# A four-layer graph stack on one core: second-layer products that share a stationary operand made one product of 256 columns

## The chip, the core and the metric

One NeuronCore of a Trainium2 chip runs the whole program. The metric is the device time of one execution in microseconds. The kernel before has a median of 750.35 us over three runs (749.72 to 751.56); lower is better.

## What is computed

The input is 64 graphs of 128 nodes with 128 features, `x`, and their adjacency matrices `adj`. Four residual layers follow each other, each after a layer norm and a ReLU: a gated recurrent graph network (five steps of message, aggregation and GRU cell), a gated graph convolution, a sum of five small graph convolutions on 25 nodes, and one normalised graph convolution. The change touches the second of them:

```
h     = relu(layernorm(x))
norm  = (sum(|adj|, -1) + 1e-6) ** -0.5
f_hom = (adj @ ((h @ theta) * norm)) * norm
f_het = h @ W_h
gate  = sigmoid(h @ W_t + b_t)
x     = x + elu(gate * f_hom + (1 - gate) * f_het)
```

The kernel uses (adj scaled) @ h first and theta afterwards, so that each graph needs four things of its normalised h (`xn`, nodes on partitions): its turn (features on partitions), the neighbour sum s = xn.T @ adjT (already turned), then h @ W_t and h @ W_h from the turned h, and s @ theta.

## The kernel before

The 64 graphs are taken in 4 rounds of 16; a round has 4 quads of 4 graphs, and 4 graphs of 128 columns fill one PSUM bank of 512 fp32 columns. The recurrent layer is the backbone: 80 steps (4 rounds, 5 layers, 4 quads), each with nine products of 512 columns on the stored state and nine on the message side, in three banks (R, Z and H or I), and the turning and aggregation of the next step's state. Each step n has two slots, 2n and 2n+1. All else is laid beside the recurrence of the next round by a table of slots: `due(slot, lead, at)` says which quad of which round a piece of work is due for. So the second layer of round r runs beside the first steps of round r+1: `turn_and_sum` (slots 0, 2, 4, 6 of that round, TURN1 = 0) and `l1_linear` (slots 1, 3, 5, 7, LINEAR1 = 1). The second layer of the last round has no recurrence beside it; it runs in a tail, where `keep_busy` (L444) puts products that nobody reads in front of waits.

Each engine has its own program and works through it strictly in the written order, with semaphores between them. On TensorE a step is: state products H, R, Z (L404 to L407), turn of the next state (L391), the even slot's work, message products R, Z, I, aggregation (L400), the odd slot's work. `turn_and_sum` stands in the even slot and `l1_linear` in the odd one.

Before the change a quad of the second layer goes like this:

- TensorE, `turn_and_sum` (L460): 4 transposes of 128 columns into the A bank (L470), then 4 fp32 products xn.T @ adjT of 128 columns into the B bank (L478). Both use the same stationary operand, `xn` of the graph. An fp32 product that is not a transpose is two instructions in the trace (a group "x8" is 4 products).
- ScalarE, `l1_read_turned` (L748): copies A to `hT` (L751) and B to `sT` (L755).
- TensorE, `l1_linear` (L482): a bias product of 512 columns into the C bank (L492), 4 products h @ W_t on top (L495), 4 products h @ W_h into A (L499), 4 products s @ theta into B (L504). L495 and L499 use the same stationary operand, `hT` of the graph.
- ScalarE, `l1_read_linear` (L757): tanh of C to `gate_th` (L762), copy of A to `hetS` (L764). Then, two slots on, `l1_exp` (L766).
- VectorE: `l1_difference` (L1195, `diff` from B and `hetS`), `l1_gate` (L1207, `gated` and `mix`), `l1_finish` (L1217). VectorE also does the `residual` of a later quad (L1181, x_res and its statistics), and the GRU arithmetic (L1359, L1362, L1352, L1335, L1343, L1348).
- GpSimd: the power of the layer norm (L936 to L946), the low halves of the state (L952, L956), `adjT` and `adjTI` scaled (L968, L992), and one large power a round (L984, `dis`).

ScalarE normalises a quad in two halves (`norm_relu`, L713), one in an even and one in an odd slot; the odd half stands behind `l1_read_linear` and `l1_exp` in its program, and the turn of that quad on TensorE waits for it.

Of the kernel before, what the change touches and what calls it, by code (L numbers as in the profile page):

```python
# [15 lines left out]
QUAD = 4  # L16
# [19 lines left out]
def graph_stack(nc, x, adj, nodemask, conv_w, w_ih, w_hh, b_ih, b_hh, theta, W_h, W_t, b_t,  # L36
# [26 lines left out]
    with ctx:  # L63
        ctx.enter_context(nc.allow_non_contiguous_dma("small transposed loads at the start"))

        def sb(name, shape, dt=f32):
# [21 lines left out]
            for n in ("fw", "fmax", "fexp", "fsum", "finv", "fshare", "b2_share"))  # L88
# [5 lines left out]
        adjT = sb("adjT", [128, RG, 128])  # L94
# [13 lines left out]
                                          for n in ("var_eps", "neg_mean", "rstd", "shift"))  # L108
# [13 lines left out]
        sT, gate_th, hetS, diff, gated, neg, ex = (sb(n, [128, 512]) for n in  # L122
                                                   ("sT", "gate_th", "hetS", "diff", "gated", "neg", "ex"))
# [28 lines left out]
            "fexp_done", "bias_rows_made",  # L152
# [183 lines left out]
        def _(pe):  # L336
# [123 lines left out]
            def turn_and_sum(r, q):  # L460

                u = r * QUADS + q
                keep_busy(r, (14, 0, 8, 5)[q])
                pe.wait_ge(sem["ln1_xn"], u + 1)
                if q:
                    pe.wait_ge(sem["l1_het"], u)
                elif r:
                    pe.wait_ge(sem["l3_y"], u)
                for j in range(QUAD):
                    last = nc.tensor.transpose(A_BANK[:, j * 128:(j + 1) * 128], xn[:, q * QUAD + j, :], ident[:])  # L470
                last.then_inc(sem["ln1_turned"], 1)
                pe.wait_ge(sem["adjT_scaled"], u + 1)
# [4 lines left out]
                for j in range(QUAD):  # L477
                    last = nc.tensor.matmul(B_BANK[:, j * 128:(j + 1) * 128], xn[:, q * QUAD + j, :],  # L478
                                            adjT[:, q * QUAD + j, :], start=True, stop=True)
                last.then_inc(sem["l1_s"], 1)  # L480

            def l1_linear(r, q):  # L482
                u = r * QUADS + q
# [6 lines left out]
                else:  # L490
                    pe.wait_ge(sem["l1_gate"], u)
                nc.tensor.matmul(C_BANK[:], ones_r[:], bias_row(0), start=True, stop=False)  # L492
                pe.wait_ge(sem["ln1_h"], u + 1)
                for j in range(QUAD):
                    last = nc.tensor.matmul(C_BANK[:, j * 128:(j + 1) * 128], hT[q % 2][:, j, :], wl1[:, 256:384],  # L495
                                            start=False, stop=j == QUAD - 1)
                last.then_inc(sem["l1_gate_lin"], 1)
                for j in range(QUAD):
                    last = nc.tensor.matmul(A_BANK[:, j * 128:(j + 1) * 128], hT[q % 2][:, j, :], wl1[:, 128:256],  # L499
                                            start=True, stop=True)  # L500
# [539 lines left out]
        def _(dve):  # L1040
# [236 lines left out]
            def beside(slot):  # L1277
# [4 lines left out]
                if slot == 7:  # L1282
                    shares()
# [110 lines left out]
```

## Time and profile before

| what | value |
|---|---|
| median of 3 runs | 750.35 us |
| the profiled execution: its own time, its span | 750.32 us, 748.5 us |
| mean granted TensorE clock | 0.992 of full |
| busy: TensorE, VectorE, ScalarE, GpSimd | 688.3, 562.1, 546.0, 300.5 us |
| idle of TensorE over the span | 60.2 us (748.5 less 688.3) |
| second layer of rounds 0, 1, 2 beside the recurrence | from 155.5, 327.4 and 499.5 us |
| second layer of the last round, in the tail | from 665.5 us |

Each engine's busy time is the sum of its instructions' own times, with overlaps counted once. A matmul's time in a row includes its way through the array, which overlaps the next one's; how long a product holds the engine is the distance to the next start, and the view of the chain shows it, since it lists the stretch that each piece takes up there.

### The profile page before, as it was taken

The page shows a single profiled execution, that of the slowest core. Times are in us where ns is not written, and L with a number is a line of the kernel's source. Part 1 is how long each engine was busy: PE and PEld are TensorE (multiplying, and loading weights), DVE is VectorE, ACT ScalarE, POOL GpSimd, SP SyncE. Part 2 cuts the span into 40 slices and gives each one's busy share as a digit, 9 for nine tenths or more (in the row PEclk, how much of TensorE's full clock was granted, in tenths as well). Part 3 has the DMA queues.
Part 4 walks back from the last instruction along what each step waited for, and adds up shares of the span by engine and source line. Part 5 has one row for each costly group of instructions (what it writes and reads, how often), then busy time and mean ns, then how long its engine had stood idle before and what let it go on. Part 6 is the DMA issues. An engine that isn't in the chain of part 4 may idle for free.

```text
span 748.5 us, 12649 instructions
## 1 busy us (share of the span) xinstructions
PE 688.3 (92%) x4198; PEld 588.4 (79%) x4198; DVE 562.1 (75%) x1398; ACT 546.0 (73%) x1147; POOL 300.5 (40%) x427
## 2 busy tenths in 40 slices
PE   2999799989999989989999989989999989988887
PEld 2788688878888778878888768878888878877665
DVE  4688976988877966888967986789876886776243
ACT  4677688578878877667878878667887777657543
POOL 4322514562344343464234443573232343553321
PEclk9999989999999999999999999999999999999999
DMA  6510011100000020410000020210000000210001
GB/s 159 147 55 1 2 48 18 52 1 4 7 3 1 1 61 11 131 29 4 6 4 1 2 60 1 71 44 4 6 4 2 1 0 1 76 39 7 6 1 56
DMA packets 47625, 21.09 MB, mean 28 GB/s; under 512 B 9033, under 2 KB 47561, under 8 KB 47561
## 3 DMA queue, kind: packets, MB, share of 16 engines
q1 hardware_dynamic: 47560, 20.29, 10.1%
q8 instruction: 34, 0.56, 0.3%
q14 instruction: 31, 0.25, 0.1%
HBM read 15.27 MB, written 4.19 MB: 26 GB/s over the span
## 4 chain that ended last, share of the span: by engine, by line
PE 49%; DVE 21%; ACT 15%; POOL 8%; issue 7%; DMA 1%; DVEq 0%; SPq 0%; POOLq 0%; ACTq 0%
PE bank L405 8%; PE bank L407 8%; PE bank L406 8%; PE bank L400 6%; DVE rh L1359 3%; ACT xn L713 3%; DVE zh L1335 2%; POOL rstd L944 2%; DVE hd L1343 2%; PE bank L391 2%; PE bank L613 2%; PE bank L543 2%; POOL dis L988 2%; PE bank L556 2%; PE bank L599 2%
## 5 line engine op out<-in xcount | busy, mean ns | idle before, releaser
L960 POOL TENSOR_TENSOR h_lo<-h,h_hi 128x512 fp32r<-128x512 f32 x64 | 84.5, 1321 | 255.1 <-ACT h_hi L893 255.1
L1359 DVE SCALAR_TENSOR_TENSOR rh<-bank,rh 128x512 f32<-128x512 f32 x80 | 55.1, 689 | 88.6 <-ACT bank L910 88.4
L405 PE MATMUL bank<-h_hi,whh_hi 128*128 128x512 f32 x240 | 105.2, 438 | 11.8 <-DVE rh L1359 11.4
L405 PE MATMUL bank<-g_hi,wc_hi 128*128 128x512 f32 x240 | 102.8, 429 | 0.0
L407 PE MATMUL bank<-h_lo,whh_hi 128*128 128x512 f32 x240 | 95.1, 396 | 0.0
L407 PE MATMUL bank<-g_lo,wc_hi 128*128 128x512 f32 x240 | 94.6, 394 | 0.0
L406 PE MATMUL bank<-h_hi,whh_lo 128*128 128x512 f32 x240 | 94.4, 393 | 0.0
L406 PE MATMUL bank<-g_hi,wc_lo 128*128 128x512 f32 x240 | 94.0, 392 | 0.0
L400 PEld LDWEIGHTS bank<-edge,hn 128*128 128x128 f32 x640 | 83.6, 191 | 8.2 <-DVE edge L1060 1.8
L400 PE MATMUL bank<-edge,hn 128*128 128x128 f32 x640 | 84.3, 274 | 1.5 <-DVE edge L1060 1.5
L713 ACT ACTIVATE xn<-x_res,shift,rstd 128x128 f32<-128x128 f32 x128 | 55.7, 485 | 31.4 <-POOL shift L946 31.4
L916 ACT ACTIVATE bank<-bank,bih 128x512 f32<-128x512 f32 x80 | 52.9, 661 | 30.1 <-DVE bank L1362 29.9
L941 POOL TENSOR_TENSOR var_eps<-mv,eps_ln 128x4 f32<-128x4 f32 (+1 forms) x64 | 17.9, 280 | 139.2 <-DVE mv L1052 125.8
L897 ACT ACTIVATE g_hi<-bank 128x512 fp32r<-128x512 f32 x80 | 47.7, 596 | 33.3 <-PE bank L400 32.9
L889 ACT ACTIVATE hn<-bank 128x512 f32<-128x512 f32 x80 | 47.6, 595 | 31.2 <-PE bank L391 30.7
L1352 DVE TENSOR_TENSOR g_lo<-bank,g_hi 128x512 fp32r<-128x512 f32 x80 | 55.0, 687 | 17.4 <-ACT g_hi L897 17.3
L405 PEld LDWEIGHTS bank<-h_hi,whh_hi 128*128 128x128 f32 x240 | 45.5, 190 | 25.1 <-DVE rh L1359 17.1
L944 POOL TENSOR_TENSOR rstd<-var_eps,neg_half 128x4 f32<-128x4 f32 (+1 forms) x64 | 59.5, 930 | 5.0
L1348 DVE SCALAR_TENSOR_TENSOR h<-zh,hd 128x512 f32<-128x512 f32 x80 | 57.0, 712 | 2.8
L1362 DVE SCALAR_TENSOR_TENSOR bank<-rh,bank 128x512 f32<-128x512 f32 x80 | 55.7, 696 | 2.7
L910 ACT ACTIVATE bank<-bank,brz 128x512 f32<-128x512 f32 x80 | 52.0, 650 | 5.3 <-PE bank L407 4.8
L903 ACT ACTIVATE rh<-bank,bhh 128x512 f32<-128x512 f32 x80 | 54.8, 684 | 0.6
(171 smaller groups left out, 1677.5 us busy)
## 6 DMA issues: line engine op xcount, KB each, us to landing
x_in<-in_x SPq DMA_DIRECT2D x8, 512.0 KB, 5.4
adj_in<-in_adj SPq DMA_DIRECT2D x8, 512.0 KB, 5.0
x_res<-in_x SPq DMA_DIRECT2D x16, 256.0 KB, 2.9
out_x<-x_res SPq DMA_DIRECT2D x16, 256.0 KB, 2.3
xz<-x_res SPq DMA_DIRECT2D x16, 50.0 KB
w_sb<-in_L_gnn_W SPq DMA_DIRECT2D x1, 640.0 KB, 5.1
w_sb<-in_L_gnn_W SPq DMA_DIRECT2D x5, 128.0 KB, 5.1
rows<-in_adj SPq DMA_DIRECT2D x32, 0.6 KB
```

The costliest lines, as they stand in the source:

```text
L400: last = nc.tensor.matmul(TG[:, j * 128:(j + 1) * 128], hn[:, j, :], edge[:, q * QUAD + j, :], start=True, stop=True)
L405: nc.tensor.matmul(dst[:], w_hi, m_hi, start=start, stop=False)
L406: nc.tensor.matmul(dst[:], w_lo, m_hi, start=False, stop=False)
L407: return nc.tensor.matmul(dst[:], w_hi, m_lo, start=False, stop=stop)
L713: last = nc.scalar.activation(dst[:, b, :], src[:, b, :], ACT.Relu, bias=shift[i][:, b:b + 1], scale=rstd[i][:, b:b + 1])
L903: nc.scalar.activation(rh[:], H_BANK[:], ACT.Identity, bias=bhh[:, 2:3]).then_inc(sem["hb_ready"], 1)
L944: nc.gpsimd.tensor_tensor(rstd[i][0:p, c], var_eps[i][0:p, c], neg_half[0:p, c], ALU.pow).then_inc(sem[f"ln{L}_pow"], 1)
L960: nc.gpsimd.tensor_tensor(h_lo[q][:], h[q][:], h_hi[q][:].bitcast(f32), ALU.subtract).then_inc(sem["h_lo_new"], 1)
L1348: nc.vector.scalar_tensor_tensor(h[q][:], zh[:], 0.5, hd[:], ALU.mult, ALU.subtract).then_inc(sem["h_new"], 1)
L1352: nc.vector.tensor_tensor(g_lo[:], TG[:], g_hi[:].bitcast(f32), ALU.subtract).then_inc(sem["g_lo_ready"], 1)
L1359: nc.vector.scalar_tensor_tensor(rh[:], R_BANK[:], 1.0, rh[:], ALU.add, ALU.mult).then_inc(sem["rh_ready"], 1)
L1362: nc.vector.scalar_tensor_tensor(I_BANK[:], rh[:], 0.5, I_BANK[:], ALU.mult, ALU.add).then_inc(sem["pre_ready"], 1)
```

## The change

The turn is no longer a transpose. `adjT` gets a seventeenth slot that holds the identity, and one fp32 product per graph streams the graph's scaled adjacency and the identity (a strided pair of 128 columns each) past the stationary `xn`: 256 columns, of which 128 are the sum s and 128 the turned h. Two graphs fill a bank: graphs 0 and 1 of the quad go to A, graphs 2 and 3 to B. ScalarE copies each bank into a buffer `sh` with s and h side by side, of which there are two. The linear part streams W_h and W_t together (256 columns) past the turned h; the bias goes in as a last product of 2 x 128 columns into each of two banks, A for the first pair of graphs and C for the second. s @ theta stays as it was. ScalarE reads gate and het from each of the two banks, so two instructions of 512 columns become four of 256. The wait for the scaled adjacency moves ahead of the first product, and the wait of the copy to `sT` for the last s @ theta goes, as there are two buffers. One copy of the identity on VectorE is added in slot 7 of the first round.

```diff
-        adjT = sb("adjT", [128, RG, 128])
+        adjT = sb("adjT", [128, RG + 1, 128])
...
+        sh = [sb(f"sh{i}", [128, QUAD, 256]) for i in range(2)]
...
                 keep_busy(r, (14, 0, 8, 5)[q])
+                pe.wait_ge(sem["identity_beside"], 1)
                 pe.wait_ge(sem["ln1_xn"], u + 1)
+                pe.wait_ge(sem["adjT_scaled"], u + 1)
...
-                for j in range(QUAD):
-                    last = nc.tensor.transpose(A_BANK[:, j * 128:(j + 1) * 128], xn[:, q * QUAD + j, :], ident[:])
+                for j in range(2):
+                    b = q * QUAD + j
+                    last = nc.tensor.matmul(A_BANK[:, j * 256:(j + 1) * 256], xn[:, b, :], adjT[:, b:RG + 1:RG - b, :],
+                                            start=True, stop=True)
                 last.then_inc(sem["ln1_turned"], 1)
-                pe.wait_ge(sem["adjT_scaled"], u + 1)
...
-                for j in range(QUAD):
-                    last = nc.tensor.matmul(B_BANK[:, j * 128:(j + 1) * 128], xn[:, q * QUAD + j, :],
-                                            adjT[:, q * QUAD + j, :], start=True, stop=True)
+                for j in range(2):
+                    b = q * QUAD + 2 + j
+                    last = nc.tensor.matmul(B_BANK[:, j * 256:(j + 1) * 256], xn[:, b, :], adjT[:, b:RG + 1:RG - b, :],
+                                            start=True, stop=True)
                 last.then_inc(sem["l1_s"], 1)
...
-                else:
-                    pe.wait_ge(sem["l1_gate"], u)
-                nc.tensor.matmul(C_BANK[:], ones_r[:], bias_row(0), start=True, stop=False)
-                pe.wait_ge(sem["ln1_h"], u + 1)
+                for pair, dst, read, made in ((0, A_BANK, "ln1_h", "l1_gate_lin"), (2, C_BANK, "l1_s_read", "l1_het_lin")):
+                    pe.wait_ge(sem[read], u + 1)
+                    if q and pair:
+                        pe.wait_ge(sem["l1_het"], u)
+                    for j in range(2):
+                        nc.tensor.matmul(dst[:, j * 256:(j + 1) * 256], sh[q % 2][:, pair + j, 128:256], wl1[:, 128:384],
+                                         start=j == 0, stop=False)
+                    nc.tensor.matmul(dst[:].rearrange("p (b d) -> p b d", b=2)[:, :, 128:256], ones_r[:],
+                                     bias_rows[:, 0, :].unsqueeze(1).to_broadcast([128, 2, 128]), start=False, stop=True
+                                     ).then_inc(sem[made], 1)
                 for j in range(QUAD):
-                    last = nc.tensor.matmul(C_BANK[:, j * 128:(j + 1) * 128], hT[q % 2][:, j, :], wl1[:, 256:384],
-                                            start=False, stop=j == QUAD - 1)
-                last.then_inc(sem["l1_gate_lin"], 1)
-                for j in range(QUAD):
-                    last = nc.tensor.matmul(A_BANK[:, j * 128:(j + 1) * 128], hT[q % 2][:, j, :], wl1[:, 128:256],
-                                            start=True, stop=True)
-                last.then_inc(sem["l1_het_lin"], 1)
-                pe.wait_ge(sem["l1_s_read"], u + 1)
-                for j in range(QUAD):
-                    last = nc.tensor.matmul(B_BANK[:, j * 128:(j + 1) * 128], sT[:, j * 128:(j + 1) * 128], wl1[:, 0:128],
+                    last = nc.tensor.matmul(B_BANK[:, j * 128:(j + 1) * 128], sh[q % 2][:, j, 0:128], wl1[:, 0:128],
                                             start=True, stop=True)
                 last.then_inc(sem["l1_hom"], 1)
...
             def l1_read_turned(r, q):
                 u = r * QUADS + q
+                if u >= 2:
+                    act.wait_ge(sem["l1_hom"], u - 1)
                 act.wait_ge(sem["ln1_turned"], u + 1)
-                nc.scalar.activation(hT[q % 2][:], quad(A_BANK[:, :]), ACT.Copy).then_inc(sem["ln1_h"], 1)
+                nc.scalar.activation(sh[q % 2][:, 0:2, :], A_BANK[:].rearrange("p (b d) -> p b d", b=2), ACT.Copy
+                                     ).then_inc(sem["ln1_h"], 1)
                 act.wait_ge(sem["l1_s"], u + 1)
-                if u:
-                    act.wait_ge(sem["l1_hom"], u)
-                nc.scalar.activation(sT[:], B_BANK[:], ACT.Copy).then_inc(sem["l1_s_read"], 1)
+                nc.scalar.activation(sh[q % 2][:, 2:4, :], B_BANK[:].rearrange("p (b d) -> p b d", b=2), ACT.Copy
+                                     ).then_inc(sem["l1_s_read"], 1)
...
-                nc.scalar.activation(gate_th[:], C_BANK[:], ACT.Tanh, scale=0.5).then_inc(sem["l1_gate"], 1)
-                act.wait_ge(sem["l1_het_lin"], u + 1)
-                nc.scalar.activation(hetS[:], A_BANK[:], ACT.Copy).then_inc(sem["l1_het"], 1)
+                for src, c in ((A_BANK, slice(0, 2)), (C_BANK, slice(2, 4))):
+                    if src is C_BANK:
+                        act.wait_ge(sem["l1_het_lin"], u + 1)
+                    pair = src[:].rearrange("p (b d) -> p b d", b=2)
+                    gate = nc.scalar.activation(quad(gate_th[:])[:, c, :], pair[:, :, 128:256], ACT.Tanh, scale=0.5)
+                    het = nc.scalar.activation(quad(hetS[:])[:, c, :], pair[:, :, 0:128], ACT.Copy)
+                gate.then_inc(sem["l1_gate"], 1)
+                het.then_inc(sem["l1_het"], 1)
...
+            def identity_beside():
+                nc.vector.tensor_copy(adjT[:, RG, :], ident[:]).then_inc(sem["identity_beside"], 1)
```

## Rows read from the trace of the kernel before

**Rows 1.** The page: span, then busy us (share) xinstructions of each engine.

```profile
span 748.5 us, 12649 instructions
PE 688.3 (92%) x4198; PEld 588.4 (79%) x4198; DVE 562.1 (75%) x1398; ACT 546.0 (73%) x1147; POOL 300.5 (40%) x427
```

**Rows 2.** TensorE's waits from 155.5 to 327.4 us, one round: total, times, longest.

```profile
PE bank L579 <- ACT rh L903: 3.2, 3, 1.6
PE bank L405 <- DVE rh L1359: 2.0, 2, 1.3
...
PE bank L470 <- ACT xn L713: 0.5, 1, 0.5
```

**Rows 3.** Chain that ended last before 200 us: start us, us, what.

```profile
153.52 3.33 POOL dis L988
...
165.92 1.14 DVE x_res L1189 x4
...
186.74 0.89 PE bank L478 x8
...
190.60 0.23 PE bank L492
...
195.59 0.44 PE bank L391 x4
```

**Rows 4.** Groups by line and shape: xcount | busy us, mean ns | idle before.

```profile
L470 PE MATMUL bank<-ident,xn 128*128 128x128 f32 x64 | 10.2, 281 | 4.6 <-ACT xn L713 4.4
...
L478 PE MATMUL bank<-adjT,xn 128*128 128x128 f32 x128 | 17.0, 276 | 0.2 <-DVE diff L1203 0.2
...
L478 PEld LDWEIGHTS bank<-adjT,xn 128*128 128x128 f32 x128 | 15.5, 192 | 0.4 <-issue 0.4
...
L532 PE MATMUL bank<-w_sb,zone 128*100 128x256 f32 x32 | 9.7, 385 | 0.3 <-ACT zone L783 0.3
```

**Rows 5.** Chain of the tail: one fp32 product of 256 columns.

```profile
697.45 0.45 PE bank L532 x2
```

**Rows 6.** Timeline of ScalarE: instructions of 512 and of 256 columns and their followers.

```profile
192.66 0.60 ACT L764 ACTIVATE hetS<-bank 128x512 f32<-128x512 f32 x1 [0.30 <-PE bank L499]
193.15 0.62 ACT L769 ACTIVATE neg<-mix 128x512 f32<-128x512 f32 x1
...
207.76 0.39 ACT L801 ACTIVATE sup<-bank 100x256 f32<-100x256 f32 x1
208.03 0.50 ACT L777 ACTIVATE xz<-xz,shift,rstd 100x128 f32<-100x128 f32 x1
```

**Rows 7.** Groups by line and shape: a VectorE copy of 128 columns.

```profile
L1237 DVE COPY sup<-bank 100x128 f32<-100x128 f32 x16 | 4.6, 285 | 5.9 <-PE bank L556 5.9
```

**Rows 8.** Timeline of TensorE ahead of the turns of quads 2 and 3.

```profile
174.95 0.60 PE L391 MATMUL bank<-ident,hx 128*128 128x128 f32 x4
176.04 0.66 PE L470 MATMUL bank<-ident,xn 128*128 128x128 f32 x4 [0.50 <-ACT xn L713]
...
185.40 0.60 PE L391 MATMUL bank<-ident,h 128*128 128x128 f32 x4
186.08 0.66 PE L470 MATMUL bank<-ident,xn 128*128 128x128 f32 x4
```

**Rows 9.** Two stretches of round 0: us, then busy of PE, PEld, DVE, ACT, POOL.

```profile
155.50:193.50 38.00, 37.42 (x262) 33.90 (x261) 32.34 (x78) 30.18 (x58) 14.69 (x23) 1.00 0.01 4
193.50:327.40 133.90, 125.00 (x759) 106.89 (x758) 105.27 (x264) 104.17 (x228) 59.71 (x82) 1.00 0.12 34
```

**Rows 10.** Chain of the tail, quads 2 and 3 of the last round.

```profile
678.36 0.66 PE bank L470 x4
...
682.45 0.63 ACT neg L769
...
684.56 0.66 PE bank L470 x4
...
689.14 1.13 DVE diff L1203 x4
```

More of the change, by code:

```diff
@@ L120, in graph_stack @@
         rh, hd, zh = sb("rh", [128, 512]), sb("hd", [128, 512]), sb("zh", [128, 512])
-        sT, gate_th, hetS, diff, gated, neg, ex = (sb(n, [128, 512]) for n in
-                                                   ("sT", "gate_th", "hetS", "diff", "gated", "neg", "ex"))
+        gate_th, hetS, diff, gated, neg, ex = (sb(n, [128, 512]) for n in ("gate_th", "hetS", "diff", "gated", "neg", "ex"))
+        sh = [sb(f"sh{i}", [128, QUAD, 256]) for i in range(2)]
         mix = [sb(f"mix{i}", [128, 512]) for i in range(2)]
@@ L151, in graph_stack @@
             "cleared", "consts", "dve_setup", "dve_turns", "w_turned", "w_turned_read", "wc_made", "wc_hi_made", "wc_lo_made",
-            "fexp_done", "bias_rows_made",
+            "fexp_done", "bias_rows_made", "identity_beside",
             "mask_round", "degs", "degs_eps", "norm1_ready", "dis_ready", "norms", "adj_turned", "adjT_ready", "adjTI_made",
@@ L553, in l2_support2 @@
                 else:
-                    pe.wait_ge(sem["l1_gate"], r * QUADS + QUADS)
+                    pe.wait_ge(sem["l1_het"], r * QUADS + QUADS)
                 for e in range(EH):
@@ L1282, in beside @@
                 if slot == 7:
+                    identity_beside()
                     shares()
```

## The prediction

> **What bounds the kernel now.** I read the page first: TensorE is busy 688.3 us of 748.5 us, VectorE and ScalarE about three quarters [rows 1]. So TensorE is the first suspect, but 60 us of its idle time are left in which other chains end last. I then read TensorE's waits for one round, from the second layer's first turn to the next round's. The reader is to see how few they are: the largest are 3.2 us at the way back of the third layer and 2.0 us for `rh`, and only one of 0.5 us stands at a turn of the second layer [rows 2]. Third, the chain around the four quads of round 0. It has two parts. Up to the turn of quad 3, at 186.1 us, it does not run on TensorE: it comes from GpSimd's large power (3.33 us at 153.52), through `xn` on ScalarE into VectorE's GRU arithmetic and its `x_res` at 165.92, and so to the turns of quads 2 and 3. From there to the aggregation that ends at 199 us it is TensorE without a break [rows 3]. The other two rounds repeat this pattern, 172 us apart. In the tail the second layer is one chain through TensorE, ScalarE and VectorE.
>
> **How long a product holds TensorE.** Row times of matmuls overlap, so I take distances of the chain. Four transposes hold it 0.44 us, four fp32 products of 128 columns 0.89 us (eight instructions), so 0.11 and 0.22 us each [rows 3]. The transpose is one instruction and the product two [rows 4]: L470 counts 64 and L478 counts 128 for the same 64 graphs. One fp32 product of 256 columns takes 0.45 us with its neighbours [rows 5]; other places of the same kind gave 0.43, and 0.44 is my value. So twice the columns cost twice the time: two products of 128 are 0.445, one of 256 is 0.44. The weight loads, 192 ns each in their rows [rows 4], do not show in the distance of 0.11 us between instructions; they are hidden under the products before them.
>
> **Turn and sum, a quad.** Removed: 4 transposes and 4 products, 0.44 + 0.89 = 1.33 us [rows 3]. Added: 4 products of 256 columns, 4 x 0.44 = 1.76 us. The cost is +0.43 us; with 0.43 a product it is +0.39. The turn was the cheap half, and it now costs as much as the sum. Sharing the stationary operand gives nothing back, as its load was hidden.
>
> The Trainium skill (Perfetto Trace Analysis, section Transposes) says that a logical transpose should be a transpose and not a standard matmul, since the array has logic that skips the arithmetic for it. By that rule the change loses here, and the trace agrees: 0.11 us against 0.22 us.
>
> **Linear part, a quad.** Removed: 8 products of 128 columns, 2 x 0.89 = 1.78 us, and one bias product of 512 columns, 0.23 us [rows 3]. Added: 4 of 256, 1.76 us, and two bias products of 256 columns. No row has one of these; below, it can't take less than half of 0.23, above it takes no more than the one of 512: 0.12 to 0.23 each. I take 0.12, as the larger one's time goes by columns (0.23 for 512). The balance is -0.02 + 0.01, about -0.01 (bounds -0.07 and +0.21). s @ theta is unchanged.
>
> Together TensorE has 0.35 to 0.43 us more a quad; I take 0.40. Sixteen quads make 6.4 us, if all of it were on the path.
>
> **ScalarE, a quad.** The reads after the turn keep their number and size (two of 512). The first can start when 2 products of 256 are through instead of 4 transposes (0.88 against 0.44 us after the start), the second at 1.76 against 1.33. Gate and het become four instructions of 256 columns. Back to back, one of 512 takes 0.49 us to the next start and one of 256 0.27 us [rows 6], so 4 x 0.27 - 2 x 0.49 = +0.10 us. Were nothing overlapped, it would be 4 x 0.39 - 2 x 0.60 = +0.36 us, the upper bound. Queued behind them are `l1_exp` and the second half of `xn`, for which the next turn waits.
>
> **Waits that are moved or added.** The wait for the scaled adjacency comes before the turn now; GpSimd scales a round's adjacency in slots 31 to 37, ahead of slot 40, and works in order, so the last of it is over when `dis` (slot 38) starts at 153.52 [rows 3]; the first turn is at 155.5. So 0, its cover being some 2 us; without it TensorE would stand in front of all its products. The read of s no longer waits for the previous s @ theta: 0, since in the trace it waits only for L478. The wait of the C bank for het is a whole step old: 0. The identity copy is one VectorE instruction in slot 7 of the first round, 0.29 us at most by its like [rows 7], once, and between 0 and 0.3 on the path; I take 0.1. No DMA is added or moved.
>
> **What reaches the end, rounds 0 to 2.** Quad 0: +0.40 on TensorE after 155.5, but the chain there is GpSimd's and VectorE's, so it is covered. Quad 1's turn comes 0.40 late and so does the turning of the state that VectorE's `x_res` at 165.92 waits for [rows 3]; VectorE shifts by something between 0 and 0.40; I take 0.25, as that turning is done just before `x_res` starts. Quad 2: TensorE would reach it 2 x 0.40 late, less the 0.50 that it waits today [rows 8] gives +0.30. By the other chain it is VectorE's 0.25 plus ScalarE's 0.10, +0.35. The later one counts: +0.35. Quad 3: today the turn starts 0.68 us after L391, whose length is 0.44, so 0.24 are in hand [rows 8]; TensorE gives 0.35 + 0.40 - 0.24 = +0.51, the other chain 0.25 + 0.2 = +0.45. With quad 3's own 0.40 the round ends +0.9 us. Three rounds: 2.7 us. If all waits shifted with TensorE, it would be 3 x 1.6 = 4.8; if the waits of later slots (8.9 us from 193.5 to 327.4, 133.9 less 125.0 [rows 9]) also took what is left, 0.
>
> **The tail.** Quad 0 gives ScalarE's +0.1, since xn of quad 1 stands behind gate and het; quad 1 the same, so the turn at 678.36 is 0.2 late. From it to `neg` at 682.45 are 4.09 us [rows 10]. After the change it is 0.22 for the start (four transposes take 0.66 after a wait instead of 0.44), 1.76, 1.76 and 0.24, so 3.98, and tanh and copy of the second pair, 0.27 each: 4.52 us, or +0.4. So quad 3's turn, 684.56, is +0.6, and its `diff` at 689.14 another +0.4: 1.0 (bounds 0.4, if the first two quads are covered and ScalarE's reads overlap, and 1.7, with 0.36 of ScalarE for each of three quads).
>
> **Sum.** 2.7 + 1.0 + 0.1 = 3.8 us on the profiled execution's 750.32 us: 754.1. Its own time is within 0.03 us of the median, so nothing is corrected. From 0.3% on (2.25 us) a difference can be told from none in this kernel: under 748.1 is faster, over 752.6 slower.
>
> **The rivals.**
> *A, all of it counts.* The four quads behave like the stretch after 186.08, with no break in TensorE's work. 16 x 0.40 = 6.4, plus 0.1: 756.8. For it: TensorE is busy 37.4 of the 38.0 us of four quads [rows 9]. Against: the chain before 186 runs elsewhere. Chance 0.20.
> *B, not slower: the waits take it.* The place is the stretch from quad 0's turn to the next round's; the mechanism is that VectorE's and GpSimd's chain sets every round's length, and TensorE's extra time only shortens its waits, which are 9.5 us a round [rows 9]. It decides if the quads' extra 1.6 us a round is less than what TensorE has in hand before the next fixed point of that chain. Then only the tail is left, 1.0, and the time is 751.3. For it: the chain of 153 to 186 us. Against: TensorE's unbroken stretch after it, and the waits for ScalarE's `rh` at L903 [rows 2], which itself waits for TensorE's first product of a step. Chance 0.17.
> *C, wide products are cheaper than their columns.* If one fp32 product of 256 columns held TensorE as long as one of 128, 0.22 us, a quad would save 0.44 + 0.89 = 1.33 us, twelve quads 16 us: 734. The row of a 256-column product, 0.45 us, speaks against it [rows 4, 5]; its stationary operand is 100 wide instead of 128, which is all that is left open. Chance 0.03.
> The Trainium skill (Perfetto Trace Analysis, section Matmuls) says that larger matmuls are more efficient than smaller ones; taken alone this rule would make the change faster, as in C, and the trace supports it only by 0.005 us a pair.
> *D, ScalarE decides.* If its four instructions cost their full 0.36 us more and each quad's turn is late by that beside TensorE's share, add 16 x 0.26 to the forecast: 758.3. Against it stand the distances of ScalarE's rows [rows 6]. Chance 0.05.
>
> **How the numbers follow.** Forecast 0.55, A 0.20, B 0.17, C 0.03, D 0.05. The forecast's own spread (0.5 to 1.5 us a round, tail 0.4 to 1.7) is 752.3 to 756.6. The range takes in A up to its bound of 0.43 a quad (16 x 0.43 + 0.1, 757.3) and most of B, from 751.2 on, and leaves C and D out. Slower: A, D and nearly all of the forecast, 0.76; same: B and the forecast's low edge, 0.20; faster: C and a little for a gain that I don't see, 0.04.
>
> **What would show it.** In the chain of the new profile the merged turn-and-sum holds TensorE 1.7 to 1.8 us a quad and the linear part without theta about 2.0; TensorE has 11 instructions fewer a quad (26 for 37); the wait of 0.5 us at quad 2's turn shrinks or goes; the start of the next round's second layer stands about 173 us after the last instead of 172; the tail after 665 us is about 1 us longer. A 256-column product at 0.22 us, or rounds still 172.0 us apart, would prove me wrong.

## The result and the profile after

The changed kernel takes 756.60 us (median of 5 runs, 755.24 to 757.30). The kernel before, run beside it, takes 750.72 us (5 runs, 749.72 to 751.56). The ratio is 1.0078, with a 95% interval of 1.0065 to 1.0091: slower by 5.9 us, where 3.8 were forecast. The profiled execution took 756.60 us itself; its span is 754.8 us, 6.3 more than before. Four executions in this document took 978 us and more (one each of e4, e5, e6 and of the kernel before, beside e9 and e10); they are left out of every median, range and ratio.

The page of the changed kernel: span, then busy us (share) and instructions of each engine.

```profile
span 754.8 us, 12343 instructions
PE 694.9 (92%) x4022; PEld 589.1 (78%) x4022; DVE 561.7 (74%) x1399; ACT 549.8 (73%) x1179; POOL 300.3 (40%) x427
```

Against [rows 1], TensorE has 176 instructions fewer (11 for each of 16 quads) and is busy 6.6 us longer. VectorE and GpSimd are unchanged within 0.4 us, and ScalarE has 32 instructions and 3.8 us more. So the engine that does most got more work in fewer instructions.

**The quad.** The chain that ended last, changed kernel, quads 0 and 3 of round 0: start us, us, what.

```profile
156.46 0.86 PE bank L473 x4
157.32 0.86 PE bank L482 x4
...
161.14 0.87 PE bank L500 x4
...
162.12 0.86 PE bank L500 x4
...
163.11 0.89 PE bank L506 x8
...
186.68 0.44 PE bank L391 x4
187.12 0.87 PE bank L473 x4
```

L473 and L482 are the merged turn and sum, L500 the merged linear part, L506 the unchanged s @ theta. An fp32 product of 256 columns holds TensorE 0.43 us (0.86 for two products, which are four instructions). Turn and sum take 1.72 us instead of 1.33 [rows 3]: +0.39. The linear part takes 0.87 + 0.11 + 0.86 + 0.13 = 1.97 us (161.14 to 163.11) instead of 2.01: -0.04. A quad costs +0.35 us. Before, this stretch of the chain was in large part GpSimd's and VectorE's; from 155.8 us on it is now TensorE's without a break through all four quads. On the page, TensorE's share of that chain has gone from 49% to 62%.

**Where the 6.3 us are.** To place them I take, in both traces, the start of the first product of `h_hi` (L405) in each of the 80 GRU steps, and subtract. The differences stay the same from step to step, within a few hundredths, except at these places (us; steps 20 to 39 and so on are rounds 0 to 2 of the second layer):

| place | changed less before |
|---|---|
| up to step 20, ahead of all changed products | +0.80 |
| quads 0, 1, 2, 3 of round 0 | +0.34, +0.35, -0.37, +0.03 |
| step 26, 46, 66: just behind quad 3 of each round | +0.97, +0.91, +0.85 |
| all three rounds (step 20 to step 79) | +4.06 |
| tail (span less step 79) | +1.4 |

So the four quads cost only 0.35 a round, as two of them gain (rounds 1 and 2 repeat the pattern), and as much as 0.9 a round comes at a place where nothing was changed. TensorE's waits of the changed kernel in one round, 155.5 to 331 us (us in total, times, longest):

```profile
PE bank L581 <- ACT rh L913: 3.2, 3, 1.6
PE bank L405 <- DVE rh L1373: 2.0, 2, 1.4
PE bank L521 <- ACT rh L913: 1.8, 1, 1.8
PE bank L457 <- ACT rh L913: 1.4, 2, 0.7
```

The same view of the kernel before, 155.5 to 327.4 us, has for the zone turn:

```profile
PE bank L519 <- ACT rh L903: 0.8, 1, 0.8
```

The first two answer to [rows 2]; the second wait at L457 belongs to the next round, as the window is 2 us longer than a round. The wait of 0.5 us at the turn is gone. The zone turn (L521; L519 before) waits 1.8 us for `rh` instead of 0.8. That is the jump of 0.97. What made `rh` late stands 6 us ahead of it. Timeline around the gate of quad 3, the kernel before (start us, us, engine, line, operation, what it waited for):

```profile
196.66 0.69 DVE L1211 SCALAR_TENSOR_TENSOR gated<-gate_th,diff 128x512 f32<-128x512 f32 x1
196.69 0.64 ACT L893 ACTIVATE h_hi<-h 128x512 fp32r<-128x512 f32 x1
...
197.39 0.69 DVE L1214 SCALAR_TENSOR_TENSOR mix<-gated,hetS 128x512 f32<-128x512 f32 x1
197.40 1.81 POOL L960 TENSOR_TENSOR h_lo<-h,h_hi 128x512 fp32r<-128x512 f32 x1 [5.97 <-ACT h_hi L893]
```

The same place in the changed kernel:

```profile
197.85 0.64 ACT L903 ACTIVATE h_hi<-h 128x512 fp32r<-128x512 f32 x1
197.87 0.69 DVE L1224 SCALAR_TENSOR_TENSOR gated<-gate_th,diff 128x512 f32<-128x512 f32 x1
...
198.57 1.28 POOL L970 TENSOR_TENSOR h_lo<-h,h_hi 128x512 fp32r<-128x512 f32 x1 [6.01 <-ACT h_hi L903]
198.59 1.80 DVE L1227 SCALAR_TENSOR_TENSOR mix<-gated,hetS 128x512 f32<-128x512 f32 x1
...
200.32 0.68 DVE L1373 SCALAR_TENSOR_TENSOR rh<-bank,rh 128x512 f32<-128x512 f32 x1
```

The reader is to see two instructions that are ready within hundredths of each other: VectorE's `mix`, which waits for the end of `gated`, and GpSimd's `h_lo`, which waits for the end of ScalarE's `h_hi`. Before, `mix` starts 0.01 us ahead and takes its usual 0.69, and `h_lo` takes 1.81. After, `h_lo` is 0.02 ahead and takes its usual 1.28 (its mean is 1.29), and `mix` takes 1.80. Who is second ends well after the first has ended, `h_lo` 1.13 us and `mix` 0.54 us after it, nearly its own length. The order hangs on 0.05 us: `h_hi` started 0.03 us behind `gated` and starts 0.02 ahead of it now. It is `gated` that moved. Counted from the start of TensorE's turn of the state (L391, 195.43 and 196.59), `h_hi` starts after 1.26 us in both kernels, `gated` after 1.23 before and 1.28 now. The 1.1 us that `mix` loses pass through VectorE's `rh` into ScalarE's queue, whose `neg`, `ex`, `xz` and `rh` (L913) are all late, and so to TensorE.

The Trainium skill (SBUF — State Buffer, section SBUF: two separate sides) says that VectorE and GpSimd share a pair of ports, which the one that starts first holds for its whole instruction while the other fully blocks; for VectorE it names, among others, instructions with two SBUF inputs, against a GpSimd instruction that reads SBUF. The rows agree with both orders: 1.81 us for `h_lo` when it is second, 1.80 for `mix`.

**Why quads 2 and 3 gain.** The same pair meets in quad 0. Timeline there, VectorE's and GpSimd's rows, the kernel before:

```profile
167.48 1.30 POOL L954 TENSOR_TENSOR h_lo<-hx,h_hi 128x512 fp32r<-128x512 f32 x1
...
167.87 1.46 DVE L1211 SCALAR_TENSOR_TENSOR gated<-gate_th,diff 128x512 f32<-128x512 f32 x1
...
169.14 1.32 POOL L960 TENSOR_TENSOR h_lo<-h,h_hi 128x512 fp32r<-128x512 f32 x1 [0.36 <-ACT h_hi L893]
169.36 1.65 DVE L1214 SCALAR_TENSOR_TENSOR mix<-gated,hetS 128x512 f32<-128x512 f32 x1
...
170.93 0.68 DVE L1359 SCALAR_TENSOR_TENSOR rh<-bank,rh 128x512 f32<-128x512 f32 x1
```

The same rows of the changed kernel:

```profile
168.30 1.29 POOL L964 TENSOR_TENSOR h_lo<-hx,h_hi 128x512 fp32r<-128x512 f32 x1
...
169.01 1.13 DVE L1224 SCALAR_TENSOR_TENSOR gated<-gate_th,diff 128x512 f32<-128x512 f32 x1
...
170.18 0.69 DVE L1227 SCALAR_TENSOR_TENSOR mix<-gated,hetS 128x512 f32<-128x512 f32 x1
...
170.68 1.32 POOL L970 TENSOR_TENSOR h_lo<-h,h_hi 128x512 fp32r<-128x512 f32 x1 [1.08 <-ACT h_hi L903]
171.25 0.69 DVE L1373 SCALAR_TENSOR_TENSOR rh<-bank,rh 128x512 f32<-128x512 f32 x1 [0.38 <-ACT bank L920]
```

Before, `gated` and `mix` both came second and took 1.46 and 1.65 us, 1.7 more than 2 x 0.69. After, `gated` is stretched by 0.44 and `mix` not at all. VectorE, 1.14 us later at `gated`, is only 0.32 us later at `rh`. With that, I read, its chain has stopped holding quads 2 and 3 [rows 8]; e6 tests it.

**The tail.** Its chain in the changed kernel, quads 2 and 3 of the last round:

```profile
683.55 1.10 PE bank L473 x4
684.65 0.86 PE bank L482 x4
685.51 1.01 PE bank L500 x4
...
690.37 1.10 PE bank L473 x4
...
695.46 1.13 DVE diff L1216 x4
```

Turn to turn are 6.82 us instead of 6.20, and the last turn to `diff` 5.09 instead of 4.58 [rows 10]: +0.62 and +0.51. The two quads ahead give the other 0.3.

My theory was then in three parts: (1) TensorE's columns, 0.35 us a quad, are the direct cost; (2) `mix` starting behind `h_lo` at quad 3 is a second cost that has nothing to do with columns, of about 0.9 us a round; (3) the collision that has gone in quad 0 is what absorbs two quads. The rivals were that step 26's jump is another effect of the change (ScalarE's four reads, or the linear part's new order), and that the direct cost is the reads' and waits', not the columns'.

### The profile page after: what moved, and what is told of

Read it like the earlier page. It is cut to its first block, busy times and chain, and to the rows that moved or that the text cites. A ratio compares the mean times of both kernels' runs of the same rounds, so it can differ in the third digit from the quotient of the medians.

```text
span 754.8 us, 12343 instructions
## 1 busy us (share of the span) xinstructions
PE 694.9 (92%) x4022; PEld 589.1 (78%) x4022; DVE 561.7 (74%) x1399; ACT 549.8 (73%) x1179; POOL 300.3 (40%) x427
## 4 chain that ended last, share of the span: by engine, by line
PE 62%; DVE 16%; ACT 13%; issue 5%; POOL 2%; DMA 1%; DVEq 0%; SPq 0%; POOLq 0%
PE bank L405 9%; PE bank L407 9%; PE bank L406 9%; PE bank L400 6%; PE bank L500 4%; PE bank L391 3%; DVE rh L1373 2%; DVE zh L1349 2%; PE bank L615 2%; ACT xn L715 2%; PE bank L473 2%; PE bank L506 2%; PE bank L482 2%; PE bank L545 2%; DVE bank L1376 2%
## 5 line engine op out<-in xcount | busy, mean ns | idle before, releaser
L970 POOL TENSOR_TENSOR h_lo<-h,h_hi 128x512 fp32r<-128x512 f32 x64 | 82.5, 1289 | 263.9 <-ACT h_hi L903 263.9
L405 PE MATMUL bank<-h_hi,whh_hi 128*128 128x512 f32 x240 | 105.8, 441 | 12.0 <-DVE rh L1373 11.6
L405 PE MATMUL bank<-g_hi,wc_hi 128*128 128x512 f32 x240 | 103.7, 432 | 0.0
L405 PEld LDWEIGHTS bank<-h_hi,whh_hi 128*128 128x128 f32 x240 | 45.8, 191 | 25.5 <-DVE rh L1373 17.3
L913 ACT ACTIVATE rh<-bank,bhh 128x512 f32<-128x512 f32 x80 | 54.9, 686 | 1.2 <-PE bank L407 0.7
```

The source lines that it names most:

```text
L405: nc.tensor.matmul(dst[:], w_hi, m_hi, start=start, stop=False)
L913: nc.scalar.activation(rh[:], H_BANK[:], ACT.Identity, bias=bhh[:, 2:3]).then_inc(sem["hb_ready"], 1)
L970: nc.gpsimd.tensor_tensor(h_lo[q][:], h[q][:], h_hi[q][:].bitcast(f32), ALU.subtract).then_inc(sem["h_lo_new"], 1)
```

## The experiments

All medians are beside the kernel before on the same chip. The changed kernel at 756.60 ran beside 750.72, so kernels are best compared by their ratios. A figure in us that is worked out from a ratio takes 750 us for the kernel before.

**e1: the changed kernel, GpSimd's h_lo of quad 3 a little later.**

```diff
             def low_half(n):
...
                 pool.wait_ge(sem["h_hi_new"], n // STEPS * SPLITS + n % STEPS + 1)
+                if n >= STEPS and n % STEPS == 3:
+                    nc.gpsimd.memset(nudge[:], 0.0)
```

> The changed kernel, with one tiny GpSimd memset (128x1) put before the low half of the state of step 3 of rounds 1 to 3, so that this h_lo starts some 0.1 us later. Theory (a race for a port): in the changed kernel this h_lo starts 0.02 us before VectorE's mix of quad 3 (198.57 against 198.59 us), mix then takes 1.80 instead of 0.69 us, and ScalarE's rh, for which the turn of the zone waits, is about 1 us late in each of three rounds. With the memset mix starts first, takes 0.7 again, TensorE's wait at the turn of the zone falls from 1.8 to 0.8 us, and the time falls by 3 x 0.9 = 2.7 us, to about 753.9. Rival (the wait comes from ScalarE's two extra instructions or from the later banks): mix may change, the wait and the time stay, 756.6 within 0.5.

Measured: 752.84 us (752.47 to 753.67), ratio 1.0039 (1.0027 to 1.0051), where the changed kernel had 1.0078. Timeline of this kernel, GpSimd's and VectorE's rows:

```profile
197.75 0.10 POOL L971 MEMSET nudge<- 128x1 f32 x1 [5.98 <-ACT h_hi L903]
...
197.80 0.69 DVE L1229 SCALAR_TENSOR_TENSOR mix<-gated,hetS 128x512 f32<-128x512 f32 x1
197.81 1.81 POOL L972 TENSOR_TENSOR h_lo<-h,h_hi 128x512 fp32r<-128x512 f32 x1
```

An added GpSimd instruction of 0.10 us makes the kernel 2.9 us faster (the ratios differ by 0.0039, x 750). `mix` is first again by 0.01 us and short, the jumps at steps 26, 46 and 66 are gone, and the quads cost 0.34, 0.34, -0.34, 0.03 as in the changed kernel. Part (2) holds: half of the loss was the collision.

**e2 and e5: the kernel before, `mix` later by a memset.** Both put a VectorE memset between `gated` and `mix` of quad 3, e2 of 1 column, e5 of 128:

```diff
             def l1_gate(r, q):
...
                 dve.wait_ge(sem["l1_gated"], u + 1)
+                if q == 3 and r + 1 < ROUNDS:
+                    nc.vector.memset(nudge[:], 0.0)
```

> The kernel before, with one tiny VectorE memset (128x1) between gated and mix of quad 3 in rounds 0 to 2. In the kernel before mix starts 0.01 us before that h_lo (197.39 against 197.40 us) and it is h_lo that is stretched, to 1.81 us. Theory (a race for a port): the memset delays mix past h_lo's start, mix takes 1.8 us, TensorE's wait at the turn of the zone grows from 0.8 to 1.8 us, and the time rises by 2.7 us to about 753.4 though nothing of the change is in it. Rival (the wait belongs to the change's own work): 750.7 to 751.0, as the memset is hidden.

> The kernel before, the VectorE memset between gated and mix of quad 3 now of 128 columns (some 0.2 us) instead of one. The small one moved mix by 0.09 us and h_lo still started 0.02 us behind it. Theory (a race for a port): now h_lo starts first, mix takes 1.8 instead of 0.69 us, TensorE's wait at the turn of the zone is 1.8 to 2.0 instead of 0.8 us in each of three rounds; 3 x 1.1 = +3.3 us, and another 1.4 us in each round in which the granted clock falls after the longer wait: 753 to 757. Rival (the wait comes with the change's own work): at most the memset's 0.2 us a round, 750.0 to 750.6.

Measured: 749.84 (ratio 0.9995, 0.9985 to 1.0005) and 749.83 us (1.0002, 0.9989 to 1.0014). Both expectations failed, and both times are near the rival's; but they say nothing on the theory, as neither edit turned the order round. From the start of `gated` to that of `mix` are 0.73 us without a memset, 0.72 in e2 and 0.74 in e5: neither memset delayed `mix` by more than 0.01 us, and the 0.09 us that the second expectation reads from e2 are not there. So e2 has `mix` at 197.95 and `h_lo` at 197.97, and e5 both at 199.64, `mix` still at 0.67 us and `h_lo` at 1.80. e9 does turn it round.

**e3 and e4: the two halves of the change by themselves.** e3 has the merged turn and sum, and reads the two halves of `sh` with the linear part of before; it waits for both reads ahead of the first product on h:

```diff
                 for j in range(QUAD):
-                    last = nc.tensor.matmul(C_BANK[:, j * 128:(j + 1) * 128], hT[q % 2][:, j, :], wl1[:, 256:384],
+                    last = nc.tensor.matmul(C_BANK[:, j * 128:(j + 1) * 128], sh[q % 2][:, j, 128:256], wl1[:, 256:384],
```

> Turn and sum merged as in the change, the linear part as in the kernel before (bias first into C, gate into C, het into A, two ScalarE reads of 512 columns). Theory (TensorE time by columns): four products of 256 in 1.72 us instead of 1.33, +0.39 a quad; the quads of a round give +0.4 to +0.8 net of waits, the tail +1.0 to 1.4, and h_lo against mix decides over another 0.9 a round, whichever way it falls: 753 if mix is first, 756 if h_lo is first. Rival (the four ScalarE reads of gate and het cost the time): without them 751 to 752.

Measured: 755.82 us (754.03 to 756.33), ratio 1.0075 (1.0063 to 1.0087). The quads of a round cost 0.40, 0.37, -0.32 and 0.09, together 0.5; there is no jump at step 26 (`mix` first at 196.93, 0.69 us). The expectation had 753 us for this order, the tail at 1.0 to 1.4, and it failed at the tail, which costs 3.3 us: the gate's four products need the h of all four graphs, half of which now comes with the second read. Its chain, e3, one quad of the tail:

```profile
667.02 0.88 PE bank L482 x4
...
667.92 0.60 ACT sh L760
...
668.66 1.13 PE bank L500 x8
```

The 0.60 us of `sh` stand open on the chain. So the two halves belong together: with the merged linear part, which starts with the pair that is read first, the tail costs 1.4 us (the changed kernel), 1.9 less.

e4 has the merged linear part, with the turn and sum and their reads of before (`hT`, `sT`):

```diff
-                nc.tensor.matmul(C_BANK[:], ones_r[:], bias_row(0), start=True, stop=False)
+                for pair, dst, read, made in ((0, A_BANK, "ln1_h", "l1_gate_lin"), (2, C_BANK, "ln1_h", "l1_het_lin")):
...
+                        nc.tensor.matmul(dst[:, j * 256:(j + 1) * 256], hT[q % 2][:, pair + j, :], wl1[:, 128:384],
+                                         start=j == 0, stop=False)
```

> Linear part merged as in the change (256 columns, two banks, bias last in each, four ScalarE reads), turn and sum as in the kernel before. Theory (TensorE time by columns): 4 x 0.86 + 2 x 0.12 ... that is 1.96 instead of 2.01 us a quad, -0.05 us, ScalarE +0.1 us a quad: 750.0 to 751.5 if mix still starts before h_lo. Rival (ScalarE's reads cost the time): 753 or more. Rival (wide products save their loads): under 749.

Measured: 755.76 us (755.11 to 758.76), ratio 1.0085 (1.0069 to 1.0100). TensorE's quads cost next to nothing, -0.07, -0.04, +0.16 and 0.00, and the tail 0.3. Yet the kernel is as slow as the whole change: the jumps at steps 26, 46 and 66 are +1.07, +2.39 and +2.45. It has the collision too (`h_lo` 199.68, 1.28 us; `mix` 199.71, 1.80 us), so it is the linear part that loses the order: from the start of the turn of the state, `gated` starts after 1.28 us in e4 as in the changed kernel, and after 1.23 in e3 as in the kernel before, while `h_hi` stands at 1.26 in all. Whether the 0.05 us come from the four reads or from the new order of the products was not tried. That two of the jumps are more than twice as large was in no theory; e9 shows why.

**e6 and e7: h_lo gives way.** e6 is the kernel before with GpSimd's `h_lo` made to wait for `mix` at both places, whatever the hundredths are; e7 is the changed kernel with the same lines:

```diff
             def first_low_half(r, q):
...
+                if r and q == 3:
+                    pool.wait_ge(sem["l1_mix"], (r - 1) * QUADS + 1)
...
             def low_half(n):
...
+                if n >= STEPS and n % STEPS == 3:
+                    pool.wait_ge(sem["l1_mix"], n // STEPS * QUADS)
```

> The kernel before, with GpSimd's low halves in the two collisions made to wait for VectorE's mix: the h_lo of quad 3's first state behind mix of quad 0 (before, gated took 1.46 and mix 1.65 us there instead of 0.69), and the h_lo of step 3 behind mix of quad 3. Theory (the collisions hold the chain): TensorE's waits of 0.5 and 0.24 us at quads 2 and 3 go, 3 x 0.7 = 2 us less, about 748. Rival (the large power on GpSimd sets that chain, not the collision): no difference, 750.0, or slower by GpSimd's later work.

> The changed kernel with the same two waits. Theory (TensorE time by columns, plus the collision): like the run with the tiny memset, 752.8, and up to 0.3 a round less from quad 0's collision, so 752.0 to 752.9. Beside the kernel before with the same waits it is 16 x 0.35 to 0.39 = 5.6 to 6.2 us slower if these waits leave TensorE nothing to hide it in, and 3 us if they do.

Measured: e6 746.42 us (745.70 to 747.93; ratio 0.9952, 0.9936 to 0.9968), e7 753.71 us (1.0049, 1.0034 to 1.0064). e6 beats both kernels, with two waits. Its timeline in quad 0, VectorE's and GpSimd's rows:

```profile
167.00 0.68 DVE L1215 SCALAR_TENSOR_TENSOR gated<-gate_th,diff 128x512 f32<-128x512 f32 x1
167.71 0.69 DVE L1218 SCALAR_TENSOR_TENSOR mix<-gated,hetS 128x512 f32<-128x512 f32 x1
...
168.54 1.29 POOL L956 TENSOR_TENSOR h_lo<-hx,h_hi 128x512 fp32r<-128x512 f32 x1 [1.87 <-DVE mix L1218]
```

All three have their short durations. The kernel gained more than expected (about 748). Against the kernel before, the gain comes at quad 2 (-0.72, -0.72, -0.70 in the three rounds) and quad 3 (-0.28, -0.30, -0.31), and 0.1 at step 46 and 66. These 0.72 and 0.3 are what the changed kernel absorbed: 0.35 - 0.72 = -0.37 and 0.35 - 0.31 = +0.04, and measured were -0.37 and +0.03. So part (3) holds: the kernel before could have had 1.0 us a round without the change.

Between e6 and e7 only the change is left: 3.1 - (-4.0) = 7.1 us of span. Rounds give 0.68 - (-3.12) = 3.8 us, 1.27 a round, the tail 1.4, and 1.85 lie ahead of step 20, where no product is changed (see below). Both expectations for e7 failed by that: it is 0.8 us above 752.9 and 7.1 us above e6, not 5.6 to 6.2; what lies in the rounds and the tail is 5.2. The quads of e7 against those of e6, round 0, cost 0.32, 0.38, 0.35, 0.31: without the collisions nothing is absorbed, and every quad pays about what TensorE's columns take (e10 tests that it is the columns).

**e8: the linear half with h_lo giving way.** e4 with the lines of e6.

> Only the linear part merged, with the same two waits. Theory: of the 6 us that this half alone showed, the collision and the clock behind it are all; without them it is within 0.5 us of the kernel before with the same waits (TensorE -0.05 us a quad, ScalarE +0.1). Rival (ScalarE's four reads or the bias at the end cost the time): 3 us or more above that kernel.

Measured: 747.48 us (746.32 to 748.06), ratio 0.9961 (0.9947 to 0.9976). From 1.0085 to 0.9961 by two waits of GpSimd. The rounds are 1.1 to 1.2 us shorter than before (e6: 0.9 to 1.1), and the tail is 0.3 longer. So the merged linear part with its four reads costs nothing in the rounds, and the interval overlaps with that of e6. Expected was at most 0.5 us above e6; by the ratios it is 0.7, within the intervals.

**e9: the kernel before, `mix` later than `h_lo`.** In the place of the memset an instruction of 0.29 us:

```diff
+                if q == 3 and r + 1 < ROUNDS:
+                    nc.vector.bn_stats(nudge[:], ident[:])
```

> The kernel before, with one bn_stats of 128 elements (0.28 us, a single SBUF input) on VectorE between quad 3's gated and mix of rounds 0 to 2. Theory of the lost start: h_lo is now the first to start when gated ends, so it takes 1.28 us and mix 1.8 us instead of 0.69; TensorE waits about 1.8 us for rh instead of 0.8; each round loses 0.28 + 1.1 less what slack there is, about 0.9 to 1.2 us: the kernel takes 753 to 754 us. Rival: the order of the two starts decides nothing and only the 0.28 us in VectorE's chain count: 750.3 to 751.2 us, and mix stays at 0.69 us.

Measured: 756.19 us (754.75 to 758.08), ratio 1.0075 (1.0060 to 1.0090). Timeline of e9, VectorE's and GpSimd's rows:

```profile
198.14 0.69 DVE L1211 SCALAR_TENSOR_TENSOR gated<-gate_th,diff 128x512 f32<-128x512 f32 x1
198.74 0.29 DVE L1214 BATCH_NORM_STATS2 nudge<-ident 128x6 f32<-128x128 f32 x1
...
198.88 1.28 POOL L960 TENSOR_TENSOR h_lo<-h,h_hi 128x512 fp32r<-128x512 f32 x1 [5.98 <-ACT h_hi L893]
198.94 1.77 DVE L1216 SCALAR_TENSOR_TENSOR mix<-gated,hetS 128x512 f32<-128x512 f32 x1
```

`mix` starts 0.80 us after `gated` instead of 0.73, which is enough. With not one product changed, the kernel before now has the same wait (1.78 to 1.79 us at L519, in all three rounds) and is as slow as the changed one. The rival, 750.3 to 751.2, is out. The loss is larger than the 3 to 4 us that the theory gave. Its jumps are +2.53, +2.56 and +0.86, and only the third has the size expected. TensorE's rows behind the wait, e9, round 0:

```profile
205.32 0.28 PE L519 MATMUL bank<-ident,xz 100*128 100x100 f32 x1 [1.78 <-ACT rh L903]
...
207.09 0.63 PE L405 MATMUL bank<-g_hi,wc_hi 128*128 128x512 f32 x1
207.51 0.63 PE L406 MATMUL bank<-g_hi,wc_lo 128*128 128x512 f32 x1
```

Stretches of e9 around it (us, busy of PE, PEld, DVE, ACT, POOL, granted TensorE clock, DMA):

```profile
204.50:206.50 2.00, 1.18 (x7) 1.15 (x8) 1.72 (x5) 1.73 (x6) 0.00 (x0) 0.93 0.00 0
206.50:208.50 2.00, 2.00 (x6) 1.51 (x6) 0.41 (x1) 1.43 (x4) 1.16 (x1) 0.50 0.09 26
208.50:210.50 2.00, 2.00 (x12) 1.72 (x11) 0.88 (x2) 0.69 (x1) 1.13 (x5) 0.72 0.00 0
```

TensorE had stood for 1.78 us, and then the granted clock fell to 0.50, 1.2 GHz, for some 3.5 us; products of 512 columns came 0.42 us apart instead of 0.23. Eight such distances make 1.5 us of the 1.7 by which the first two jumps exceed the third. In the third round, after the same 1.78 us, the clock stayed, as in all three rounds of the profiled execution of the changed kernel.

**e10: columns alone.** e6 with dummy products of 512 and 256 columns ahead of each quad's transposes, 0.35 us (the waits of e6 and one for the bias rows are left out of this cut):

```diff
+                nc.tensor.matmul(A_BANK[:], ones_r[:], bias_row(0), start=True, stop=True)
+                nc.tensor.matmul(A_BANK[:, 0:256], ones_r[:], bias_rows[:, 0, :].unsqueeze(1).to_broadcast([128, 2, 128]), start=True, stop=True)
                 for j in range(QUAD):
                     last = nc.tensor.transpose(A_BANK[:, j * 128:(j + 1) * 128], xn[:, q * QUAD + j, :], ident[:])
```

> The kernel before with GpSimd's h_lo held back behind quad 3's mix, as in the fastest run so far (746.6 us), and with one 512-column and one 256-column r product of ones and bias row (0.23 and 0.12 us, overwritten by the transposes) ahead of the transposes of each of the 16 quads: 0.35 us of TensorE time a quad, as much as the changed kernel added, and nothing else of the change. Theory that TensorE's columns alone are the cost left once the collision is gone: 0.35 us on each of 12 quads less what waits absorb is 3.8 us, the tail 1.0 to 1.5 us more: 751.0 to 752.2 us. Rival: what the changed kernel lost there comes from its reads and waits (h ready later, four reads instead of two), and TensorE time in the same place is absorbed: 747 to 748.5 us.

Measured: 752.90 us (751.16 to 754.28), ratio 1.0027 (1.0016 to 1.0038), against 753.71 and 1.0049 for the whole change in e7. The median is 0.7 us above the interval of the theory and over 4 us above the rival's. Against e6 the quads cost 0.30, 0.38, 0.35, 0.31 in round 0 and as much in the others, 3.9 us in the rounds (e7: 3.8) and 1.05 in the tail (e7: 1.4). So 0.35 us of TensorE's time a quad is enough for the whole cost that the change has in the rounds; in the tail it is 1.05 of 1.4, and the reads and the order of the products can have no more than the rest. Part (1) holds. What the time has beyond these 4.95 us lies ahead of step 20 in the profiled executions, where e10 is 2.0 us behind e6.

**The start.** Over the twelve profiled executions step 20 starts between 0.98 us earlier (e3) and 2.22 us later (e4) than in the kernel before. It does not go with the change: e1, which has all of the change, stands at -0.01, and kernels whose code differs nowhere in that part lie far apart, -0.88 (e6) and +1.48 (e9). Nor is it one number for one kernel: 17 executions of the kernel before, run beside e5 to e8, lie between 748.98 and 751.74 us. Most of it is the granted clock. The first products of 512 columns, from 23 to 24 us on, come 0.23 us apart in the kernel before and 0.42 in the changed one until 26 us, and its step 1 is 1.7 us later. In every profiled execution the clock falls to 0.50 again at 92 to 95 us, for 6.8 us in the kernel before, e1, e4, e5 and e9 and for 3.4 in the other seven; these seven get back 0.8 to 1.0 us at steps 12 and 13. What decides how long the clock is low was not tried, so I took no difference there as an effect. For the same reason the sum of the placed differences (rounds and tail) and the difference of the medians against the kernel before do not agree better than to -0.7 to +1.4 us: for the changed kernel they are 5.5 and 5.9, for e7 2.1 and 3.5, for e6 -3.1 and -3.8.

## Why the prediction was right, and where it was not

The time, 756.6, is within the range and on the side that was given 0.76. The forecast of 754.1 was 2.5 us low, and it was nearer to rival A's 756.8 than to its own; but A's mechanism, 0.40 on every quad and nothing absorbed, is not what ran: in the rounds most of the quads' cost was absorbed, and another cost took its place. (A's mechanism is what is left once both collisions are gone: e7 against e6.) That the time fell within the range is in good part luck: of the 6.3 us of span, 1.1 are the quads of the rounds, 2.7 the collision, 1.4 the tail and 0.8 the start, and the rest is too small to place; the forecast had 2.7, nothing, 1.0 and 0.1.

- **Turn and sum, +0.40 to +0.43 a quad: right.** Measured +0.39, at 0.43 us a product. Sharing the operand gave nothing back; the transposes had been the cheap half. Rival C (0.22 us a product) is out.
- **Linear part, -0.01: right in kind.** Measured -0.04, with a bias product at 0.11 and 0.13 where 0.12 was assumed. Together +0.35 instead of +0.40. e8 shows this half alone to be free in the rounds.
- **ScalarE, +0.10 a quad: right as far as its own rows go** (its reads start 0.27 us apart), and wrong in what was left out. It was costed as a delay of what stands behind it. In both kernels with the merged linear part `gated` starts 0.05 us later against `h_hi`, and that decided who waited for whom; that the four reads do this is likely and not shown.
- **The rounds, +0.9 each: the step that failed.** The forecast let the later of two shifts count at quads 2 and 3. Two things were wrong. VectorE's chain was not shifted later by 0.25 + 0.10; it came to quad 2 relatively earlier, since in quad 0 the collision with `h_lo` cost it 0.44 us instead of 1.73. And a wait is worth more than its row says: in e6 the one of 0.50 gave back 0.72, as four transposes behind a wait hold the engine 0.66 us and without one 0.44. So the quads gave 0.36 a round and not 0.9. This alone would have made the kernel better than forecast, 0.36 x 3 = 1.1 instead of 2.7.
- **A term was missing:** `mix` against `h_lo` at quad 3, 0.85 to 0.97 a round, 2.7 us in all. The forecast had no such term, and that its 0.9 a round came near the measured 1.35 is luck. e1 and e9 show this term from both sides.
- **The tail, +1.0: sized too low.** Measured +1.4; quad 2 to quad 3 gave 0.62 where 0.4 was forecast, the last turn to `diff` 0.51 instead of 0.4.
- **The waits moved, 0: right.** In the differences there is nothing ahead of the first turn of a round, and the 0.1 us of the identity copy shows nowhere (e1's step 20 stands at -0.01).
- **Rival B, the waits take it:** its mechanism was real but smaller, 1.0 of 1.4 us a round, and e6 shows that it was no merit of the change. Rival D is out: e8.

What was in view and was passed over: VectorE's `gated` took 1.46 us in quad 0 of the kernel before, and the same line took 0.69 in quad 3. Where one line of one shape has two durations, a collision is the first thing to look for.

## What to carry to other kernels

Before TensorE products are merged to share a stationary operand, look whether its load shows at all: here 256 columns cost twice 128, and a merge that turns a transpose into half of a product costs 0.1 us for each one (0.43 against 0.11 + 0.22). In a kernel where VectorE and GpSimd both work on SBUF, look for rows of one line with two durations, and let the less urgent of the two wait on a semaphore of the other, rather than leave the order to hundredths of a microsecond: that was worth 3.6 us to the kernel before (0.5%), and the change, which measured +0.8% by chance of order, measured +0.5% with it. Judge a change by a place-by-place difference of two traces: the net difference can be made of a gain and a loss at places that the change does not touch.

## What the runs showed of the hardware that I had not expected

- A start of 0.01 or 0.02 us earlier decides whether VectorE's 512-column instruction takes 0.69 or 1.80 us, GpSimd's being 1.81 or 1.28. An instruction of 0.10 us in the right place gave 2.9 us back (e1), one of 0.29 us in the wrong place took 5.6 (0.0075 x 750, e9, falls of the clock included).
- After TensorE had waited 1.8 us the granted clock fell to 0.50 in four cases (e4 and e9, two rounds each) and not in others of the same length (all three in the changed kernel, one each in e4 and e9). A round with such a fall lost 1.3 to 1.7 us more than the same kernel's round without one. What tells the cases apart is open; it was not tried.
- A VectorE memset of 0.17 us between two dependent instructions delayed the second by 0.01 us (e5): its row, 199.56 to 199.73, overlaps the end of the first and the start of the second.
